# Whole-quad evictions, a four-tile b2 product and normalization on ScalarE in a macaron block

## What is computed

```python
def ffn(x):                                   # 8 experts, top 2, hidden 256
    probs = softmax(x @ gate_w.T + gate_b)
    topk_vals, topk_idx = top_k(probs, 2)
    h = relu(einsum('bsd,edh->bseh', x, w1) + b1)
    expert_out = einsum('bseh,eho->bseo', h, w2) + b2
    sel = take_along_axis(expert_out, topk_idx[..., None], axis=2)
    return sum(sel * topk_vals[..., None], axis=2)
def attn(x):                                  # 8 heads of 32
    q = x @ Wq.T; k = (x @ Wkv_down.T) @ Wk_up.T; v = (x @ Wkv_down.T) @ Wv_up.T
    return softmax(q @ k.T * 32 ** -0.5) @ v @ Wo.T
x = x + 0.5 * ffn(layernorm(x))               # stage A
x = x + attn(layernorm(x))                    # stage B
x = x + 0.5 * ffn(layernorm(x))               # stage C
```

## Time and profile before

| | |
|---|---|
| median of 3 runs | 1470.93 us |
| profiled execution, device time | 1466.14 us |
| its span, first to last instruction | 1464.3 us |
| mean granted TensorE clock | 0.931 of full speed |
| busy: TensorE, VectorE, ScalarE, GpSimd | 1281, 936, 652, 794 us |

### The profile page before, as it was taken

The page is one execution under the profiler, slowest core; times in us unless marked ns, Lnnn a source line. Parts: engine busy times, 40 slices in busy tenths (PEclk is TensorE's granted clock), DMA queues, the critical chain, the costliest instruction groups (busy, mean ns, idle before and its releaser), DMA issues.

```text
span 1464.3 us, 29417 instructions
## 1 busy us (share of the span) xinstructions
PE 1281.1 (87%) x10269; PEld 905.2 (62%) x10269; DVE 936.1 (64%) x2518; ACT 652.4 (45%) x1297; POOL 794.0 (54%) x783
## 2 busy tenths in 40 slices
PE   3888888899878998989999999989978898997885
PEld 1666564676656666665766666666655666575574
DVE  4665658766477777675784865676567865653133
ACT  0223443553545544544455444545544455543431
POOL 1023646525666745665557665467675526736633
PEclk9978898999999999999999998999988999998897
DMA  9115463545454524445652654344334253473761
GB/s 317 73 37 182 141 196 109 155 150 170 128 155 126 168 84 141 144 140 181 176 166 73 188 156 142 92 132 135 114 114 134 68 152 112 146 224 125 216 212 53
DMA packets 173653, 209.73 MB, mean 143 GB/s; under 512 B 17402, under 2 KB 116418, under 8 KB 173508
## 3 DMA queue, kind: packets, MB, share of 16 engines
q1 hardware_dynamic: 152672, 172.79, 38.2%
q0 software_dynamic: 15360, 31.49, 7.4%
q10 hardware_dynamic: 5476, 3.59, 0.8%
HBM read 159.04 MB, written 48.76 MB: 142 GB/s over the span
## 4 chain that ended last, share of the span: by engine, by line
PE 44%; DVE 22%; POOL 12%; issue 9%; DMA 9%; ACT 3%; ACTq 1%; POOLq 0%; SPq 0%; DVEq 0%
PE act_ring L1429 26%; PE dve_ring L1429 11%; DVE neg_m L1384 8%; POOL pairs L930 5%; DMA Y<-results_C,posC 5%; DVE X L1364 4%; POOL Y L981 4%; PE dve_ring L1654 3%; DMA slots_A<-xnA,posA 2%; POOL slots_C L961 2%; PE act_ring L1525 1%; ACT probs L1050 1%; POOL slots_A L961 1%; DMA Y<-results_A,posA 1%; DVE nat_l L1251 1%
## 5 line engine op out<-in xcount | busy, mean ns | idle before, releaser
L1384 DVE TENSOR_REDUCE neg_m<-dve_ring 128x1 f32<-128x512 f32 x512 | 317.4, 681 | 135.0 <-PE dve_ring L1429 121.2
L930 POOL TENSOR_TENSOR pairs<-probs 128x512 f32<-128x512 f32 x256 | 321.0, 1278 | 64.1 <-ACT probs L1050 60.6
L1050 ACT ACTIVATE probs<-act_ring 128x512 f32<-128x512 f32 x512 | 264.4, 603 | 140.7 <-PE act_ring L1429 124.6
L961 POOL DMA_INDIRECT slots_A<-xnA,posA x120 | 117.8, 981 | 243.8 <-DVE posA L1348 88.6
L1429 PE MATMUL act_ring<-wt,hg 128*128 128x128 f32 x1352 | 205.9, 295 | 0.0
L1429 PE MATMUL act_ring<-xg_T,wt 128*128 128x128 f32 x1352 | 189.1, 291 | 6.8 <-DMA wt<-packed 2.7
L1429 PEld LDWEIGHTS act_ring<-xg_T,wt 128*128 128x128 f32 x1352 | 173.7, 203 | 30.6 <-issue 15.4
L981 POOL DMA_INDIRECT Y<-results_C,posC x120 | 114.7, 956 | 135.6 <-DMA Y<-results_C,posC 91.2
L1429 PEld LDWEIGHTS act_ring<-wt,hg 128*128 128x128 f32 x1352 | 185.5, 199 | 0.1
L1429 PE MATMUL dve_ring<-nat_h 32*128 32x512 f32 x512 | 140.2, 502 | 44.4 <-DVE neg_m L1384 13.9
L961 POOL DMA_INDIRECT slots_C<-xnC,posC x120 | 117.3, 978 | 109.8 <-DMA slots_C<-xnC,posC 35.2
(11 more groups left out here) (200 smaller groups left out, 2263.3 us busy)
## 6 DMA issues: line engine op xcount, KB each, us to landing
wt<-packed SPq DMA_DIRECT2D x338, 320.0 KB
xs<-slots_A SPq DMA_DIRECT2D x37, 256.0 KB
results_A<-ys SPq DMA_DIRECT2D x37, 256.0 KB
xs<-slots_C SPq DMA_DIRECT2D x37, 256.0 KB
results_C<-ys SPq DMA_DIRECT2D x37, 256.0 KB
X<-in_L_attn_x_dram SPq DMA_DIRECT2D x16, 256.0 KB, 5.2
out_dram<-X SPq DMA_DIRECT2D x16, 256.0 KB
packed<-probs SPq DMA_DIRECT2D x1, 2560.0 KB, 8.1
```

What stands on the lines that cost most here:

```text
L930: pool.tensor_tensor(pairs[:, kt // 2, j, :], probs[:, kt - 1, j, :], probs[:, kt, j, :], ALU.add).then_inc(S["p_added"], 1)
L961: pool.indirect_dma_start(out=slots[s][:], out_offset=bass.IndirectOffsetOnAxis(ap=pos[s, c % C_RING][:, k, t:t + 1], axis=0), in_=xn[s][: ...
L1050: act.activation(probs[:, kt, j, :], act_ring[(before + j) % A_RING][:], ACT.Exp, scale=SCALE).then_inc(a_done, 1)
L1384: V_.tensor_reduce(neg_m[:, g, n, j:j + 1], dve_ring[(before + j) % D_RING][:], AX.X, ALU.max, negate=True).then_inc(d_done, 1)
```

## The change

Three edits and a new plan.

1. The four banks of a ring become one PSUM tensor (`dve_banks`, `act_banks`). A `max` is evicted by one TENSOR_REDUCE over 4 x 512 columns and an `s` by one exponential over 2048 columns. TensorE signals once at the end of the last product, and all four banks are handed back together. Which head lies in which bank now follows the ring's position.
2. `scaled`: VectorE makes the refined 1/sqrt and `shift`, for all three stages, and signals `shift_done`; the four 128x128 instructions run on ScalarE as ACTIVATE Identity with per-row scale and bias.
3. `y` begins with one b2 product over the quad's tiles (512 or 384 columns) where it had one of 128 columns per tile. For this the quad's weights lie side by side: the ring of 8 weight tiles becomes 2 quads of 4 (`W_QUADS`, `w_place`).
4. The planner's numbers and three costs change, and with them the order on every engine.

```diff
-W_RING, XS_RING, ... = 8, 3, ...
+W_QUADS, XS_RING, ... = 2, 3, ...
...
-PERIOD, FIRST_B = 37.27, 78.18
+PERIOD, FIRST_B = 37.29, 109.19
...
             def wload(at):
...
-                if i >= W_RING:
-                    s0, c0, i0 = tiles_in_turn[i - W_RING]
-                    sp.wait_ge(a_full, counts["a_full", (s0, c0, "y", i0 // 4)])
+                turn = quad_turn[s, c, tile // 4]
+                if turn >= W_QUADS:
+                    s0, c0, q0 = quads[turn - W_QUADS]
+                    sp.wait_ge(a_full, counts["a_full", (s0, c0, "y", q0)])
...
+            def scaled(at):                      # ScalarE
+                s, b = at.stage, at.index
+                act.wait_ge(S["shift_done"], at.count("shift_done"))
...
+                if s == "B":
+                    wait(act, d_full, at.count("d_full", "xT", index=b - 1))
+                for n in range(TILES):
+                    last = act.activation(xn[s][:, xn_place(s, b) + n, :], X[:, b % X_RING, n, :], ACT.Identity,
+                                          bias=shift[s][:, n:n + 1], scale=rstd[s][:, n:n + 1])
+                last.then_inc(S["xn_done"], 1)
...
             def s_(at):                          # ScalarE
...
-                for j in range(GROUP):
-                    act.wait_ge(a_full, before + j + 1)
-                    act.activation(probs[:, kt, j, :], act_ring[(before + j) % A_RING][:], ACT.Exp, scale=SCALE).then_inc(a_done, 1)
+                act.wait_ge(a_full, before + GROUP)
+                act.activation(probs[:, kt, :, :], act_banks[:], ACT.Exp, scale=SCALE).then_inc(a_done, GROUP)
...
             def scaled(at):                      # VectorE
...
-                if at.stage == "B":
-                    for n in range(TILES):
-                        last = V_.tensor_scalar(xn["B"][:, n, :], xb[:, n, :], mv["B"][:, n, 0:1], r[:, n:n + 1],
-                                                ALU.subtract, ALU.mult)
...
+                plus = shift[at.stage]
+                wait(dve, S["xn_done"], at.count("xn_done", index=at.index - 1))
+                chain(V_.tensor_tensor(plus[:], mv[at.stage][:, :, 0], r[:], ALU.mult))
+                V_.tensor_scalar(plus[:], plus[:], -1.0, 0.0 if at.stage == "B" else 1.0, ALU.mult, ALU.add).then_inc(S["shift_done"], 1)
...
             def max_(at):                        # VectorE
...
-                for j in range(GROUP):
-                    dve.wait_ge(d_full, before + j + 1)
-                    V_.tensor_reduce(neg_m[:, g, n, j:j + 1], dve_ring[(before + j) % D_RING][:], AX.X, ALU.max,
-                                     negate=True).then_inc(d_done, 1)
+                dve.wait_ge(d_full, before + GROUP)
+                V_.tensor_reduce(neg_m[:, g, n, :], dve_banks[:], AX.X, ALU.max, negate=True).then_inc(d_done, GROUP)
...
             def y(at):                           # TensorE
...
+                pe_mm(bank[:, 0:len(tiles) * D].rearrange("p (i d) -> p i d", d=D), b2_rows[:],
+                      wt[:, first:first + len(tiles), B2C:WCOLS], stop=False)
...
-                    pe_mm(dst, b2_rows[:], wt[:, i, B2C:WCOLS], stop=False)
...
             def max_(at):                        # TensorE, s_ alike
...
-                        last = pe_mm(dve_ring[(before + j) % D_RING][:], q[rows, g, 0, tokens(n)], k[rows, g, 1, :],
-                                     start=p == 0, stop=p == 2)
-                        if p == 2:
-                            last.then_inc(d_full, 1)
+                        last = pe_mm(dve_ring[j], q[rows, g, 0, tokens(n)], k[rows, g, 1, :], start=p == 0, stop=p == 2)
+                last.then_inc(d_full, GROUP)
```

111 lines of the change are left out of this document (57 added, 54 removed), and 2 rows, old and new, of the table PARTS.

## The result

The changed kernel takes 1531.76 us (median of four runs, 1530.07 to 1535.63) beside 1477.42 us of the kernel before in the same session (1462.93 to 1483.98): a ratio of 1.0385, 95% interval 1.0294 to 1.0477. The profiled execution spans 1533.9 us at a mean granted clock of 0.897, before 1464.3 us at 0.931. The forecast was 1455 us, 1422 to 1488. It missed its range on the slow side. The profiled execution of the kernel before was one of its quicker ones: 69 further executions average a span of 1468.9 us and a clock of 0.925.

The account below looks back on a forecast made before the run. The prediction took TensorE's list as the main bound, but not alone, with GpSimd's indirect pairs pacing the last 269 us. Terms -15 + 0 + 10 - 8 = -13 from 1466.1 gave 1453, set at 1455 us, range 1422 to 1488.

Parts of the forecast that it names:

- The new order: Every engine's list of steps: same pattern and work, places move by a few steps; 0, with +-15 for waiting engines.
- The merged evictions' length: ScalarE and VectorE over four banks: exponentials 1.92 us for 2.06, maxima 2.27 us for 2.48.
- Their refill: TensorE refilling four banks after a merged eviction: periods 3.34 us (maxima) and 3.23 (exponentials); together 0, bounds -11 and +10.
- The forecast's own mark: Sign of being wrong: TensorE waits over 100 us more in sum for probs and neg_m.
- The held banks: Single-bank TensorE steps behind an s or max get their bank later: +10 us, bounds 0 and +68.
- slower: held banks: Rival: single-bank steps wait 1.2 to 1.6 us more at up to 58 places, 1511 us; 13% for loss beyond 2%.
- The b2 product: TensorE's y steps: one product per quad saves 0.21 us (four tiles) or 0.16 (three); -15 us, bounds -20 and -9.
- nothing happens: Rival: TensorE's saved 20 us become waits for GpSimd's pairs and the rest cancels, 1466 us; chance 0.16.
- ScalarE's scaling: Normalization moved from VectorE to ScalarE: VectorE's relief outweighs ScalarE's cost and later hand-over; -8 us, bounds -19 and +8.
- late rows: Rival: scaled on ScalarE comes 0.5 us later in each of 48 steps, +24 in place of -8, 1485 us; 11%.
- The clock: TensorE's mean clock 0.931, 14% of time at the lower level, where b2 saves double: 17.8 us becomes 20.
- The tail: From 1195 us to the end, GpSimd's 52 indirect DMA pairs at 5.2 us set the pace, unaffected by the change.

Follow-up runs that it names:

- Two nudges of 0.3 us: Kernel before, instructions unchanged, sixteen B_SHIFT planner numbers moved 0.3 us up and down in turn, then with signs reversed: ratios 1.0371 and 1.0215.
- one replan for the weights: Kernel before with the b2 product per quad and weights handed over by quads, planned anew: 1499.9 us, ratio 1.0177.
- a_undone: Changed kernel's planner and order with all three instruction edits undone, weights still in two quads: 1527.1 us, ratio 1.0349 against the kernel before.
- b_wait_all: Kernel before, order kept, single evictions; TensorE waits until all four banks are handed back before a quad's first pass: 1486.6 us, ratio 1.0104.
- b_joint: Kernel before with the merged evictions alone, order kept: 1483.0 us, ratio 1.0098.
- b_start_all: Kernel before, order kept, single evictions; VectorE and ScalarE start a quad's evictions only when all four banks are full: 1485.2 us, ratio 1.010.
- b_b2_same: Kernel before with the b2 product per quad in exactly the old order: 1470.8 us, ratio .9983.

## Why the prediction was wrong, point by point

**The new order, counted as 0 +-15: the step that failed.** The forecast took likeness of the lists ("the same pattern with the same work; places move by a few steps") for likeness of time. Only 504 of TensorE's 972 steps stand in the old sequence. Measured, +51 us with the old instructions, and +22 (give or take 18) beside all three edits. Two nudges of 0.3 us and one replan for the weights gave +54, +32 and +26 us, so none of four other orders came out within 15 us. A trace of one order could not give the size, but the planner could have given a part: priced at the old costs, the new order ends 33 us later. The runs show where the loss sits (ahead of 814 us, at C's fourth routed chunk). By the table, 30 of a_undone's 55 us of span are full-clock time, with longer waits on GpSimd, and 25 are the clock's. Why the new order misses even the model's time stays open; no run isolated one place in the order.

**The merged evictions' length: right.** Forecast 1.92 us for the exponentials and 2.27 for the maxima, measured 1.877 and 2.291.

**Their refill, counted as 0 (-11 to +10): mis-sized.** The steps of the sum were 3.34 us for a period of maxima and 3.23 for one of exponentials; measured are 3.53 and 3.33 as medians at the higher level, against 3.31 and 3.12. The signal takes 0.15 us and not 0.05, the passes 1.08 and not 1.02. The 0.05 for the signal had no row behind it. That makes 0.2 us a pair, some 15 us for the changed kernel's 29 + 41 pairs of under 3.6 us, and another 37 pairs take about 4.21 us. b_wait_all, which loses the early refill alone, costs 15 us, above the bound of 10. The forecast's own mark, 100 us more of TensorE waiting, is passed by the products (+136) and nearly by the weight loads (+97). But it was a poor mark, as b_joint shows: +117 and +72 with 14 us lost.

**The held banks, +10 (0 to +68).** In the old order nothing of them shows beside the refill (b_joint 14 us, b_wait_all 15). Beside the other edits the merge costs 31 us in either order; how much of the further 17 is held banks was not isolated. The rival "slower: held banks", 1511 us, had the right sign, and the wrong place for most of the loss.

**The b2 product, -15: right in size, wrong on where it counts.** The group has x74 and x14, 88 in all. A y of four tiles now shows this on the weight loads (timeline of the changed kernel):

```profile
708.67 0.19 PEld L1442 LDWEIGHTS act_banks<-wt,b_rows 128*128 128x128 f32 x1 [0.84 <-issue]
708.78 1.99 PEld L1442 LDWEIGHTS act_banks<-wt,hg 128*128 128x128 f32 x16
```

From the first load to the last one's start are 0.11 + 1.99 - 0.19 = 1.91 us; with the pitch of the earlier trace rows it was 4 x 0.56 - 0.11 = 2.13. That is 0.22 us a quad, forecast 0.21. In the new order it gave 17 us. In the old one it gave 3, which its interval can't tell from 0: TensorE's busy time fell by 14 us (1267.6 for 1281.1) and the average span did not follow, as in the rival "nothing happens", but for this edit only.

**ScalarE's scaling, -8 (-19 to +8): small, its sign not settled.** +6 us in the old order (2 to 10); -10 in the new, which is within the noise of the two ratios. The step's duration was wrong: 483 ns an instruction, where the estimate from rows was 273, and four take 1.65 us (timeline of the changed kernel), not 0.8.

```profile
608.59 1.65 ACT L1045 ACTIVATE xnC<-X,shiftC,rstdC 128x128 f32<-128x128 f32 x4 [2.91 <-DVE shiftC L1256]
```

The Trainium skill, "ScalarE: Activation LUTs", section "What ACT_TABLE_LOAD costs", has the figures from which the prediction worked out an estimate of about 480 ns and 1.6 us a step, since both the scale and the bias are per-partition operands; the trace agrees with it. Rows of instructions without such operands could not show this. ScalarE's 192 instructions take 79 us, not 38. VectorE's busy time fell by 66 us, not 56 + 26. The rival "late rows" (+24) came at most in part, +6 in the old order.

**The clock was not in the sum.** The forecast used it only as a factor on the b2 products. By the table the clock's part grew from 111 to 157 us, 46 of the changed kernel's 62 us of span. In the two profiled executions it grew by 57 us, 36 of them while TensorE was busy and the rest while it stood idle at the lower level, so the 46 are an upper bound. b_joint has 4 us more full-clock time and 9 more in the clock's part (7 and 7 against the kernel before of its own session). All three edits in the old order leave the full-clock part as it was (1357 for 1358), where the forecast's sum said 13 less, and the clock's part grows by 40.

**The sum as measured.** By ratios on 1466 us: order +51; b2 and scaled in it -26 (1.0349 to 1.0171); merge +31 (1.0171 to 1.0385): +56, with +-13 on the last ratio alone, and the two merges +-14 and +-16. Read in the other sequence: b2 and scaled +3, merge +31, then the order +22. The parts depend on what is there already, and neither sequence is the right one. What both say is that the merge costs some 30 us beside the other two edits, and the order 22 to 51.

**The tail: right.** 52 pairs in 266 us, 5.1 us each.

## What to carry to other kernels

An edit that makes a planner lay the program out anew is two edits: time the old instructions in the new order, and the new instructions in the old order, before the gain or loss is put down to the instructions. Ask the planner's model too, and at one set of costs for both orders: an end that got earlier because the costs got lower says nothing of the order. Merging evictions of a ring saves fixed costs on the evicting engine, but the ring is then handed over in lumps, both ways; here 0.2 us more per hand-over came with a lower granted clock (.919 for .925 in b_joint) and 1% lost. Put the clock in the sum as a term of its own: split the span into c x span and (1 - c) x span, average it over several executions, and ask of each edit what it does to TensorE's pauses.

## What the runs showed of the hardware that was not expected

- The granted clock fell in the three kernels that differ from the kernel before only in filling, evicting or handing back a quad's banks in lumps (b_joint .919, b_wait_all .918, b_start_all .919, the kernel before .925), in b_start_all with no more idle time in its profile (174 us for 183). It rose where products were added in the same places (.940, and .938 on top of b_b2_same's .922). The passes of a max stand 0.22 us apart at the higher level and 0.42 at the lower, about the two to one of 2.4 and 1.2 GHz. What precisely TensorE has to have done before it falls was not isolated.
- One maximum over 2048 columns in four banks takes 2.291 us and one exponential 1.877 us. The former is 0.19 us shorter than four single ones, the latter 0.18.
- From the end of such an eviction to the first product that waited for it: 0.15 us.
- An ACTIVATE of 128 columns with scale and bias per partition takes 483 ns; one of 256 columns without takes 383.
- Those ACTIVATEs took 477 to 495 ns each, all 192 of them. The TENSOR_SCALARs of the kernel before that they replace took about 340 ns in the median on VectorE, but up to 3.09 us; the one step of 3.84 us ran beside additions on GpSimd.
